# Attention 0 of a fused decoder kernel: moving the transposes of context and input between the fill slots

## The chip, the cores and the metric

The kernel runs on one core of one Trainium2 chip. The metric is device time in microseconds of one execution. Lower is better.

## The reference

The program computes four blocks one after the other on x (16 batches of 100 rows, 256 features) and a context (16 batches of 361 rows, 256 features), all in float32. Block 0 is a decoder layer: causal self-attention with 16 heads, a layer norm, cross-attention to the context, a layer norm, a GELU feed-forward, a layer norm. Blocks 1 and 2 follow with further attentions, feed-forwards and a recurrence, block 3 with a target attention. What the change touches is the first attention of block 0, cut from the reference:

```python
q = jnp.einsum('bsd,hed->bhse', xq, Wq) + bq[None, :, None, :]
k = jnp.einsum('bsd,hed->bhse', xk, Wk) + bk[None, :, None, :]
v = jnp.einsum('bsd,hed->bhse', xv, Wv) + bv[None, :, None, :]
s = jnp.einsum('bhqe,bhke->bhqk', q, k) * (1.0 / math.sqrt(D_MODEL))
if causal:
    s = jnp.where(mask, s, -jnp.inf)
w = jax.nn.softmax(s, axis=-1)
o = jnp.einsum('bhqk,bhke->bhqe', w, v)
...
sa = _mha(q, k, v, m_Wq, ..., causal=True)
x = _ln(x + sa, ln1_g, ln1_b)
```

## The kernel before

The kernel keeps x and the context transposed, features on the partitions, in x_resid and ctx_t. Each of the two 128-feature halves of a tensor is a "part" (c = 0, 1). Batches are worked on one by one, and projections for a group of 4 batches at once (400 columns). The five attentions are called s0, c0, s1, c1, c2; s0 is attention 0.

The order of the work is written out by hand. ORDER gives for each attention the tokens of one batch, and every engine walks through the same string and issues its own share at each token. For batch b in s0: P are the values products of batch b-1 (pe_values), R the scores of batch b with their exp on ScalarE (pe_scores, act_probs), T the "tops", bf16 scores of batch b+1 whose maxima VectorE takes (pe_tops, dve_maxima), V the values projection of b+1, X the turn of the maxima (pe_turn, dve_rows). n0 and n1 are the two halves of batch b-1's normalisation: on ScalarE n0 copies the second heads, on VectorE n0 is two sums, a shuffle and a reciprocal (L1458 to L1465), and n1 the product that writes q_then_o (L1471). GpSimd follows no tokens; it cuts the causal triangle out of the probabilities (L1879) and writes the masked queries (L1869) batch by batch.

F is a fill slot. In s0 a batch has 5 of them, a group 20, numbered from 0. At each F an engine takes one step of several generators that run together (pe_fill, act_fill, dve_fill):

- pe_unload and act_unload turn the context of the group's batches and the x of the next group: TensorE transposes from the staging tile (L460 context, L450 x), ScalarE copies to ctx_t and x_resid (L1021);
- pe_post, from slot POST_AT["s0"] = 3 on, works on the group before: two output projections, then the norm's mean and variance. The first of them waits for n1 of that group's last batch;
- pe_pre, from slot PRE_AT["s0"] on, makes queries and keys of the next group (q0, q1, k0, k1);
- in the last group, pe_open from slot 12 on begins the next attention, c0: queries, keys of batch 0, values and tops, keys of batch 1.

The slots before are, within a group: 1 context 0; 3 x part 0, out 0; 4 context 1, out 1; 6 x part 1, mean; 7 context 2; 9 variance, q0; 10 context 3, q1; 11 k0; 12 k1; 13 to 19 nothing. A context here is both of its parts.

Results of projections, turned maxima and transposes go to a ring of three PSUM banks, 4, 5 and 6; each take waits until the reader of the bank's last content is done. Attention c0 has bank 6 alone for its projections, and pairs of banks (0, 2 and 4) for its tops and keys. The context's staging tile has room for two batches: on SyncE load_ctx waits for the second part of batch b before it loads batch b+2, and load_x waits for the second part of x.

Of the kernel before, what the change touches and what calls it, by code (L numbers as in the profile page):

```python
# [10 lines left out]
ACT = mybir.ActivationFunctionType  # L11
# [4 lines left out]
P = 128  # L16
DC = D // P
GB = 4
NG = B // GB
# [99 lines left out]
for a in ATT.values():  # L119
# [22 lines left out]


ORDER = {
# [5 lines left out]
}  # L150
POST_AT = {"s0": 3, "c0": 0, "s1": 2, "c1": 0, "c2": 6}
PRE_AT = {"s0": 9, "c0": 4, "s1": 4, "c1": 3, "c2": 1}
NORM_OF = {"s0": "n1", "c0": "n2"}
AFTER = {"f0": "c0", "f1": "s1", "f2": "c1"}
FINAL = ("c2", B - 1)
NORM_AFTER = {"f0": "n3", "f2": "r1"}

S0_OPEN = 6
TAIL_AT, CLOSE_AT, LAST_AT = 12, 1, 3

OPEN_AT = ((0, 0, 0, 0), (0, 1, 2, 4), (0, 1, 4, 1))
# [34 lines left out]
def build(nc, book, x_in, ctx_in, vec_in, const_in, src_in, w0_in, w1_in, w2_in, tw_in, out, spill):  # L196
    known = book.known
    with ExitStack() as ctx:
# [98 lines left out]
        def mark(track, point, by=1):  # L297

            counts[track] += by
            book.marks[point] = (track, counts[track])  # L300
            book.totals[track] = counts[track]
            return by
# [141 lines left out]
        def pe_x(pe, g, c, ring):  # L444

            if due(f"x{g}"):
                pe.wait_ge(sems["x_loaded"], at(f"x{g}"))
            bk = ring.take(pe, f"xt{g} {c}", f"xt{g} {c} out")
            for b in range(GB):
                i = nc.tensor.transpose(PS[:, bk, b * S:(b + 1) * S], XST[0:S, b, c * P:(c + 1) * P], IDENT[0:S, 0:S])  # L450
            i.then_inc(products_ready, mark("pe", f"xt{g} {c}"))

        def pe_ctx(pe, b):

            if due(f"ctx{b}"):
                pe.wait_ge(sems[f"ctx{b % 2}_loaded"], at(f"ctx{b}"))
            for c in range(DC):
                bk = lin["s0"].take(pe, f"ct{b} {c}", f"ct{b} {c} out")
                for kc, (k0, kn) in enumerate(KCH):
                    i = nc.tensor.transpose(PS[:, bk, k0:k0 + kn], CST[0:kn, b % 2, kc, c * P:(c + 1) * P], IDENT[0:kn, 0:kn])  # L460
                i.then_inc(products_ready, mark("pe", f"ct{b} {c}"))

        def source(t, g):
            return XN[g] if t == "c2" else X[:, :, cols(g)]
# [169 lines left out]
        def later(slots, part):  # L634
            for _ in range(slots):
                yield
            yield from part
# [66 lines left out]
        def pe_unload(pe, g):  # L704

            for b in range(g * GB, (g + 1) * GB):
                pe_ctx(pe, b)
                yield
                yield
                if b % GB < DC and g + 1 < NG:  # L710
                    pe_x(pe, g + 1, b % GB, lin["s0"])
                yield

        def pe_fill(pe, t, g):

            parts = []
            if t == "s0":
                parts.append(later(1, pe_unload(pe, g)))
            if g or t == "c0":
                parts.append(later(POST_AT[t], pe_post(pe, *((t, g - 1) if g else ("s0", NG - 1)), lin["c2 fill" if t == "c2" else t])))  # L720
            elif t == "s1":
                parts.append(pe_chain(pe, "n3", NG - 1, lin[t]))
            if t == "c2" and g + 1 == NG:
                parts.append(later(TAIL_AT, pe_chain(pe, "r2", 0, lin["c2 fill"])))
            if g + 1 < NG:
                parts.append(later(PRE_AT[t], pe_pre(pe, t, g + 1)))
            elif t == "s0":
                parts.append(later(12, pe_open(pe, "c0")))
            return together(*parts)
# [293 lines left out]
        def act_x(act, g, c):  # L1023
            act_evac(act, f"xt{g} {c}", X[:, c, cols(g)], func=ACT.Copy)
            mark_same(f"s0 in{g} {c}", f"xt{g} {c} out")

        def act_ctx(act, b):
            for c in range(DC):
                act_evac(act, f"ct{b} {c}", CT[:, b, c, :], n=C, func=ACT.Copy)

        def act_query(act, t, g, m, which="q"):
            use = f"{t} {which}{g} {m}"
# [139 lines left out]

        def act_unload(act, g):
            for b in range(g * GB, (g + 1) * GB):
                act_ctx(act, b)
                yield
                yield
                if b % GB < DC and g + 1 < NG:
                    act_x(act, g + 1, b % GB)
                yield  # L1180

        def act_fill(act, t, g):
            parts = []
            if t == "s0":
                parts.append(later(1, act_unload(act, g)))
            if g or t == "c0":
                of, og = (t, g - 1) if g else ("s0", NG - 1)
                if of in NORM_OF:
                    parts.append(later(POST_AT[t] + 3, act_chain(act, NORM_OF[of], og)))
            elif t == "s1":  # L1190
                parts.append(act_chain(act, "n3", NG - 1))
            if t == "c2" and g + 1 == NG:
                parts.append(later(TAIL_AT, act_chain(act, "r2", 0)))
            if g + 1 < NG:
                parts.append(later(PRE_AT[t], act_pre(act, t, g + 1)))
            elif t == "s0":
                parts.append(later(12, act_open(act, "c0")))
            return together(*parts)
# [935 lines left out]
```

## Time and profile before

| | us |
|---|---|
| median of 3 runs | 1598.15 |
| lowest and highest | 1595.85, 1599.1 |
| the profiled execution | 1599.62 |
| its span | 1597.2 |
| PE busy in the span | 1528.3 |
| DVE busy | 775.5 |
| ACT busy | 668.6 |
| POOL busy | 263.0 |

Times in the profile are microseconds from the start of the span. PE is TensorE's matmuls and transposes, PEld its weight loads, DVE VectorE, ACT ScalarE, POOL GpSimd, SPq the queue of SyncE, which issues all DMAs. L435 is line 435 of the kernel; many projections share it. A float32 projection of one 128-feature half is four matmul rows. In timelines instructions of the same line are merged (x4), with the start of the first and the time to the end of the last; matmuls overlap, so prices are best taken from start to start. In brackets stands the idle time of the engine before the row and what ended it. PEclk is the granted TensorE clock as a share of 2.4 GHz: 0.50 is 1.2 GHz, and values between are a mixture of both.

### The profile page before, as it was taken

How to read it: one execution, taken by the hardware profiler on the slowest of the kernel's cores; microseconds unless marked ns; L12 is line 12 of the kernel's file. 1: busy time of each engine (PE TensorE's matmuls, PEld its weight loads, DVE VectorE, ACT ScalarE, POOL GpSimd, SP SyncE). 2: the span in 40 equal slices, each digit the busy share in tenths (PEclk: the TensorE clock that was granted, in tenths of full speed). 3: DMA queues.
4: the chain of work that ended last, by engine and by line, in shares of the span. 5: the costliest groups of instructions: out<-in, count | busy, mean ns of one | idle time of the engine just before them, and what ended most of it. 6: DMA issues, size and time to landing. Idle time of an engine off the chain costs nothing.

```text
span 1597.2 us, 28533 instructions
## 1 busy us (share of the span) xinstructions
PE 1528.3 (96%) x12168; PEld 983.1 (62%) x12168; DVE 775.5 (49%) x1568; ACT 668.6 (42%) x1401; POOL 263.0 (16%) x443
## 2 busy tenths in 40 slices
PE   8899899999999999999999999999899999999997
PEld 7556556666665556555577765555466666655575
DVE  1577667677652235411133342233777777762132
ACT  2455546556564443211243341223554444443243
POOL 1333301010000001000022220000154454410000
PEclk9989989999999999999999999999999999999999
DMA  4311000000000020000020000000000000020032
GB/s 157 101 49 38 20 27 2 2 1 2 2 2 27 0 80 1 21 1 0 0 80 1 1 2 27 0 0 7 27 1 2 2 2 1 2 78 0 0 94 59
DMA packets 19551, 36.83 MB, mean 23 GB/s; under 512 B 2048, under 2 KB 17376, under 8 KB 18272
## 3 DMA queue, kind: packets, MB, share of 16 engines
q1 hardware_dynamic: 19424, 35.01, 6.6%
q8 instruction: 95, 1.56, 0.4%
q14 instruction: 32, 0.26, 0.1%
HBM read 33.36 MB, written 1.64 MB: 22 GB/s over the span
## 4 chain that ended last, share of the span: by engine, by line
PE 83%; DVE 11%; ACT 3%; issue 1%; DMA 1%; POOL 0%; SPq 0%; DVEq 0%; ACTq 0%
PE psum L435 38%; PE psum L792 11%; PE psum L486 8%; PE psum L597 6%; PE psum L558 5%; DVE maxima L1426 3%; PE psum L524 3%; PE psum L897 2%; PE psum L554 2%; DVE denoms L1465 2%; PE psum L925 1%; PE psum L938 1%; PE psum L906 1%; DVE t L1536 1%; PE psum L890 1%
## 5 line engine op out<-in xcount | busy, mean ns | idle before, releaser
L435 PE MATMUL psum<-x_resid,weights 128*128 128x400 f32 x832 | 294.9, 505 | 6.1 <-ACT probs L1100 1.9
L1426 DVE TENSOR_REDUCE maxima<-psum 100x2 f32<-100x722 f32 (+3 forms) x332 | 245.1, 759 | 111.5 <-PE psum L524 95.0
L435 PEld LDWEIGHTS psum<-x_resid,weights 128*128 128x128 f32 x832 | 156.5, 191 | 124.7 <-issue 4.5
L1100 ACT ACTIVATE probs<-psum 128x800 f32<-128x800 f32 (+3 forms) x224 | 168.0, 788 | 106.2 <-PE psum L558 105.0
L792 PE MATMUL psum<-weights 128*128 128x400 f32 x512 | 174.8, 499 | 0.7 <-DVE maxima L1426 0.7
L435 PE MATMUL psum<-weights,ctx_t 128*128 128x256 f32 (+1 forms) x576 | 158.2, 399 | 1.7 <-ACT values L1071 1.0
L792 PEld LDWEIGHTS psum<-weights 128*128 128x128 f32 x512 | 97.2, 190 | 75.1 <-DVE maxima L1426 0.8
L486 PE MATMUL psum<-ctx_t,weights 128*128 128x361 f32 x384 | 140.1, 490 | 1.9 <-DVE weights L1657 0.8
L435 PEld LDWEIGHTS psum<-weights,ctx_t 128*128 128x128 f32 (+1 forms) x576 | 100.4, 186 | 42.5 <-issue 10.8
L1021 ACT ACTIVATE weights<-psum 128x400 f32<-128x400 f32 (+2 forms) x80 | 38.0, 475 | 209.1 <-PE psum L435 209.1
L558 PE MATMUL psum<-q_masked,keys 32*128 32x200 f32 (+4 forms) x1408 | 123.9, 340 | 0.0
L1071 ACT ACTIVATE values<-psum 128x256 f32<-128x256 f32 (+2 forms) x176 | 67.8, 385 | 125.4 <-PE psum L435 90.4
L597 PE MATMUL psum<-probs,values 128*32 128x100 f32 (+5 forms) x3328 | 112.5, 253 | 0.9 <-DVE q_then_o L1484 0.3
L1864 POOL TENSOR_TENSOR q_masked_bf<-q_then_o,ones 128x200 bf16<-128x200 f32 x48 | 25.2, 527 | 507.4 <-ACT q_then_o L1021 445.2
L558 PEld LDWEIGHTS psum<-q_masked,keys 32*128 32x128 f32 (+4 forms) x1408 | 105.7, 184 | 1.2
L1657 DVE TENSOR_TENSOR weights<-psum,weights 128x400 f32<-128x400 f32 x64 | 36.8, 574 | 138.0 <-PE psum L435 119.7
L597 PEld LDWEIGHTS psum<-probs,values 128*32 128x32 f32 (+5 forms) x3328 | 85.4, 114 | 22.1 <-issue 19.2
L486 PEld LDWEIGHTS psum<-ctx_t,weights 128*128 128x128 f32 x384 | 71.2, 198 | 36.0 <-issue 9.3
L1021 ACT ACTIVATE weights<-psum,vectors 128x400 f32<-128x400 f32 x80 | 46.2, 592 | 96.5 <-PE psum L435 95.4
L1437 DVE TENSOR_TENSOR max_rows<-psum,constants 128x400 bf16<-128x400 f32 (+1 forms) x80 | 39.0, 488 | 80.5 <-PE psum L532 79.9
L524 PE MATMUL psum<-keys_bf,q_masked_bf 32*100 32x361 bf16 (+1 forms) x448 | 65.0, 358 | 11.6 <-DVE maxima L1426 6.5
L1536 DVE RECIPROCAL t<-t 128x400 f32<-128x400 f32 x20 | 52.9, 2647 | 45.9 <-ACT t L1121 45.9
(151 smaller groups left out, 2168.1 us busy)
## 6 DMA issues: line engine op xcount, KB each, us to landing
weights<-in_w SPq DMA_DIRECT2D x2, 3072.0 KB, 10.1
staged<-in_ctx SPq DMA_DIRECT2D x32, 128.0 KB, 2.1
values<-in_ctx SPq DMA_DIRECT2D x32, 128.0 KB, 2.1
weights<-in_w SPq DMA_DIRECT2D x3, 1024.0 KB, 4.9
weights<-in_src SPq DMA_DIRECT2D x1, 2368.0 KB, 14.7
weights<-in_w SPq DMA_DIRECT2D x1, 2048.0 KB, 9.0
weights<-in_tw SPq DMA_DIRECT2D x2, 1024.0 KB, 4.9
staged<-in_ctx SPq DMA_DIRECT2D x16, 105.0 KB, 2.3
```

The costliest lines, as they stand in the source:

```text
L435: i = nc.tensor.matmul(PS[0:rows, bk, 0:n], lhs, rhs, start=k == 0, stop=k == len(terms) - 1)
L486: i = nc.tensor.matmul(PS[:, bk + m, 0:C], w(WN[t][1], c, m * P, (m + 1) * P), CT[:, b, c, :], start=c == 0, stop=c == DC - 1)
L524: i = nc.tensor.matmul(PS[0:S, bk + d, 0:C], queries_bf(t, b, i0 + d, c, e), keys_bf(t, b, i0 + d, c, e), start=True, stop=True)
L558: i = nc.tensor.matmul(PS[0:kn, bk + d, m * n:(m + 1) * n], keys_of(t, b, i0 + d, c, a["keys"][kc][0], kn), queries_of(t, b, i0 + d, c), s ...
L597: mm = nc.tensor.matmul(PS[head_rows(t, i, e), bk, o:o + S], lhs, probs_of(t, b, i, c, kc, kn, e), start=kc == 0, stop=kc == lastk)
L792: i = nc.tensor.matmul(PS[:, bk, 0:N], w(wd, k, m * P, (m + 1) * P), hidden[:, k, :], start=k == 0, stop=k == 7)
L1021: nc.scalar.activation(out, PS[0:rows, bank(use), 0:n], func, **kw).then_inc(act_results, mark("act", point or f"{use} out"))
L1071: nc.scalar.activation(dst, src, ACT.Copy).then_inc(act_results, mark("act", f"{use} out"))
L1100: nc.scalar.activation(PT[0:kn, k % PROBS_KEPT, :, 0:n], PS[0:kn, bk:bk + 2, 0:n], ACT.Exp).then_inc(act_results, mark("act", f"{t} p{b} { ...
L1426: nc.vector.reduce_max(top, src, AX).then_inc(dve_results, mark("dve", f"{t} m{b} {j}"))
L1437: nc.vector.tensor_tensor(MB[:, b % 2, 0:n * S].rearrange("p (s q) -> p s q", s=n), PS[:, bank(f"{t} mt{b}"), 0:S].unsqueeze(1).broadcast_ ...
L1536: nc.vector.reciprocal(rs, rs).then_inc(dve_results, mark("dve", f"{n} rs{g}"))
```

## The change

In s0 the third fill slot of a batch moves ahead of n1. The unload generators run over five slots for each batch instead of a first slot left out and three for each batch: the two x parts of the next group are turned in slots 1 and 2 of a group's first batch, and each batch's own context in that batch's slots 3 and 4, one part in each. PRE_AT goes from 9 to 11, so that q0, q1, k0 and k1 stand in slots 11 to 14. The slots of post and of the opening of c0 stay.

```diff
@@ -142,20 +142,23 @@
 ORDER = {
-    "s0": "P0 P1 F n0 R0 R1 F n1 F T0 T1 F F V0 X",
+    "s0": "P0 P1 F n0 R0 R1 F F n1 T0 T1 F F V0 X",
...
-PRE_AT = {"s0": 9, "c0": 4, "s1": 4, "c1": 3, "c2": 1}
+PRE_AT = {"s0": 11, "c0": 4, "s1": 4, "c1": 3, "c2": 1}
...
+SLOTS_S0, CTX_AT, X_AT = 5, (3, 4), ((0, 1), (0, 2))
...
-        def pe_ctx(pe, b):
+        def pe_ctx(pe, b, c):
 
             if due(f"ctx{b}"):
                 pe.wait_ge(sems[f"ctx{b % 2}_loaded"], at(f"ctx{b}"))
-            for c in range(DC):
-                bk = lin["s0"].take(pe, f"ct{b} {c}", f"ct{b} {c} out")
-                for kc, (k0, kn) in enumerate(KCH):
-                    i = nc.tensor.transpose(PS[:, bk, k0:k0 + kn], CST[0:kn, b % 2, kc, c * P:(c + 1) * P], IDENT[0:kn, 0:kn])
-                i.then_inc(products_ready, mark("pe", f"ct{b} {c}"))
+            bk = lin["s0"].take(pe, f"ct{b} {c}", f"ct{b} {c} out")
+            for kc, (k0, kn) in enumerate(KCH):
+                i = nc.tensor.transpose(PS[:, bk, k0:k0 + kn], CST[0:kn, b % 2, kc, c * P:(c + 1) * P], IDENT[0:kn, 0:kn])
+            i.then_inc(products_ready, mark("pe", f"ct{b} {c}"))
...
         def pe_unload(pe, g):
 
             for b in range(g * GB, (g + 1) * GB):
-                pe_ctx(pe, b)
-                yield
-                yield
-                if b % GB < DC and g + 1 < NG:
-                    pe_x(pe, g + 1, b % GB, lin["s0"])
-                yield
+                for slot in range(SLOTS_S0):
+                    for c in range(DC):
+                        if g + 1 < NG and (b % GB, slot) == X_AT[c]:
+                            pe_x(pe, g + 1, c, lin["s0"])
+                        if slot == CTX_AT[c]:
+                            pe_ctx(pe, b, c)
+                    yield
...
-                parts.append(later(1, pe_unload(pe, g)))
+                parts.append(pe_unload(pe, g))
```

The act_ctx, act_unload and act_fill of ScalarE change in the same way.

## Rows read from the trace of the kernel before

**Rows 1.** The page, part 4: the chain that ended last, by engine

```profile
PE 83%; DVE 11%; ACT 3%; issue 1%; DMA 1%; POOL 0%; SPq 0%; DVEq 0%; ACTq 0%
```

**Rows 2.** Table of stretches, one a batch of attention 0 (0-6, 8, 12-15)

```profile
core 0: us, PE busy (x) PEld busy (x) DVE busy (x) ACT busy (x) POOL busy (x), PEclk, DMA share, GB/s
42.19:48.15 5.96, 5.86 (x63) 4.10 (x62) 2.31 (x5) 3.52 (x7) 3.39 (x4) 1.00 0.84 305
48.15:60.15 12.00, 10.24 (x92) 6.63 (x92) 6.31 (x9) 4.62 (x9) 3.51 (x4) 0.72 0.47 153
60.15:70.14 9.99, 9.82 (x96) 5.97 (x95) 5.78 (x9) 6.42 (x13) 3.51 (x4) 1.00 0.12 37
70.14:77.86 7.72, 4.98 (x78) 3.18 (x77) 6.04 (x9) 2.71 (x6) 3.51 (x4) 1.00 0.02 4
77.86:91.66 13.80, 13.80 (x103) 9.14 (x102) 7.47 (x11) 4.48 (x9) 3.51 (x4) 0.63 0.17 55
91.66:101.55 9.89, 9.82 (x101) 6.42 (x100) 6.08 (x11) 7.24 (x13) 3.52 (x4) 1.00 0.28 80
101.55:111.54 9.99, 9.83 (x96) 5.98 (x96) 9.26 (x12) 8.11 (x15) 3.47 (x4) 1.00 0.12 37
...
119.27:130.38 11.11, 11.01 (x103) 7.53 (x102) 7.81 (x11) 4.38 (x9) 3.52 (x4) 0.85 0.24 68
...
157.98:168.78 10.80, 10.68 (x98) 7.15 (x97) 6.49 (x11) 3.86 (x8) 3.52 (x4) 0.84 0.23 69
168.78:177.22 8.44, 8.17 (x93) 5.35 (x92) 6.07 (x11) 6.41 (x11) 3.51 (x4) 1.00 0.01 4
177.22:191.31 14.09, 12.63 (x100) 7.50 (x99) 8.74 (x12) 8.84 (x16) 1.76 (x2) 0.88 0.00 1
191.31:209.75 18.44, 14.64 (x95) 7.72 (x94) 12.05 (x16) 5.08 (x12) 6.76 (x8) 0.72 0.00 1
```

**Rows 3.** Timeline of TensorE in batch 3: start, time, what, idle before

```profile
70.14 0.89 PE L597 MATMUL psum<-probs,values 100*32 100x100 f32 x32
70.97 0.37 PE L554 MATMUL psum<-max_rows,ones_bf 32*100 32x400 bf16 x2
...
73.05 0.51 PE L512 MATMUL psum<-scan_state,ident_bf 100*100 100x400 bf16 x2 [0.81 <-ACT probs L1100]
...
74.59 1.11 PE L435 MATMUL psum<-weights,x_resid 128*100 128x256 f32 x4
77.63 0.30 PE L532 MATMUL psum<-constants,maxima 100*128 100x100 f32 x1 [1.93 <-DVE maxima L1426]
```

**Rows 4.** TensorE in 2 us of batch 4: busy, granted clock

```profile
80.00:82.00 2.00, 2.00 (x11) 0.50 0.00 0
```

**Rows 5.** Timelines of SyncE's queue and of TensorE in batches 0 and 1

```profile
44.26 4.12 SPq L1957 DMA_DIRECT2D staged<-in_ctx  x6
...
52.49 1.47 PE L460 MATMUL psum<-constants,staged 128*128 128x128 f32 x6 [1.76 <-DMA staged<-in_ctx]
```

**Rows 6.** Timeline of TensorE in batches 5 and 6, for prices

```profile
93.68 0.56 PE L450 MATMUL psum<-constants,staged 100*128 100x100 f32 x4
94.08 1.53 PE L435 MATMUL psum<-t,ones_mean 128*128 128x400 f32 x4
...
102.37 0.84 PE L460 MATMUL psum<-constants,staged 128*128 128x128 f32 x6
103.06 1.52 PE L435 MATMUL psum<-x_resid,weights 128*128 128x400 f32 x4
...
105.71 2.95 PE L435 MATMUL psum<-x_resid,weights 128*128 128x400 f32 x8
```

**Rows 7.** Timelines of GpSimd and VectorE: n1 in batches 7 and 12

```profile
114.37 1.76 POOL L1879 TENSOR_SCALAR_AFFINE_SELECT probs<-probs 100x800 f32<-100x800 f32 x2 [2.78 <-ACT probs L1100]
115.97 1.21 DVE L1471 TENSOR_TENSOR q_then_o<-second_heads,denoms 128x200 f32<-128x200 f32 x1
...
163.07 0.39 DVE L1471 TENSOR_TENSOR q_then_o<-second_heads,denoms 128x200 f32<-128x200 f32 x1
```

**Rows 8.** Timelines of TensorE and VectorE in batches 14 and 15

```profile
184.70 2.52 PE L435 MATMUL psum<-x_resid,weights 128*128 128x400 f32 x4 [0.72 <-ACT q_then_o L1021]
...
198.00 2.19 DVE L1471 TENSOR_TENSOR q_then_o<-second_heads,denoms 128x200 f32<-128x200 f32 x1
...
204.42 5.02 PE L486 MATMUL psum<-ctx_t,weights 128*128 128x361 f32 x8 [0.28 <-DVE maxima L1426]
```

More of the change, by code:

```diff
@@ L1025, in act_x, with act_ctx @@
             mark_same(f"s0 in{g} {c}", f"xt{g} {c} out")
-        def act_ctx(act, b):
-            for c in range(DC):
-                act_evac(act, f"ct{b} {c}", CT[:, b, c, :], n=C, func=ACT.Copy)
+        def act_ctx(act, b, c):
+            act_evac(act, f"ct{b} {c}", CT[:, b, c, :], n=C, func=ACT.Copy)
         def act_query(act, t, g, m, which="q"):
@@ L1174, in act_unload @@
             for b in range(g * GB, (g + 1) * GB):
[L1175 to L1180, printed above, removed]
+                for slot in range(SLOTS_S0):
+                    for c in range(DC):
+                        if g + 1 < NG and (b % GB, slot) == X_AT[c]:
+                            act_x(act, g + 1, c)
+                        if slot == CTX_AT[c]:
+                            act_ctx(act, b, c)
+                    yield
         def act_fill(act, t, g):
@@ L1184, in act_fill @@
             if t == "s0":
-                parts.append(later(1, act_unload(act, g)))
+                parts.append(act_unload(act, g))
             if g or t == "c0":
```

## Prediction

> **What bounds the kernel now.** I read the page first, then a table of stretches cut at the batches of attention 0, then the timelines of TensorE, VectorE, ScalarE and GpSimd inside them. The page's chain of the work that ended last is 83% PE and 11% DVE [rows 1]: TensorE's stream sets the time wherever it is full, VectorE where it runs dry. The change touches only attention 0, 167.56 us from 42.19 to 209.75; I cut it where TensorE starts a batch's values products (tokens P0 P1) [rows 2]. Two kinds of batch stand there.
>
> Batch 3 (and 7 and 11, 7.73 and 7.72 us) has no fill at all: TensorE is busy for 4.98 of 7.72 us. It waits 0.81 us for the first exp before the next batch's tops (T0), and 1.93 us for the maxima before the turn (X) [rows 3]. What sets 7.72 is a loop through VectorE: values, ScalarE's copies of the second heads, n0 with its reciprocal, n1, two maxima, turn, values. Batches 2, 5 and 6 are the other kind: TensorE 9.82 or 9.83 of 9.89 or 9.99 us, that is full.
>
> Two losses follow. The DVE loop leaves the array idle in batches 3, 7 and 11, and in batches 4, 8 and 12, which follow them, the mean granted clock is 0.63, 0.85 and 0.84, part of each at the lower level of 1.2 GHz: 80 to 82 us shows 0.50 [rows 2, 4]. And in batch 1 TensorE waits 1.76 us for the DMA of the context, then runs at the lower clock too (0.72) [rows 2, 5]. That load is issued at 44.26, while the queues move 305 GB/s (the 2 MB of ff weights go first), and wanted eight us later [rows 5].
>
> **Prices at the full clock.** From start to start, less the waits: values 0.83, scores 1.27, tops 1.54, V 1.11, X 0.23, which is batch 3's 4.98 [rows 3]. In a full stream the tail of V runs beside the next row, so I count the bare batch at 4.8. Both context parts of a batch together 0.69 (102.37 to 103.06), an x part 0.40 (93.68 to 94.08), a projection of 400 columns 1.40 (105.71 to 108.50 for two) [rows 6]. Out, mean, var, q0, q1, k0, k1 are all such projections. Batch 5 checks it: 4.8 + 0.4 + 1.4 + 0.7 + 1.4 + 1.4 = 10.1 against 9.89.
>
> **Part 1, the DVE order.** On TensorE and ScalarE "F n1 F" and "F F n1" are the same stream, since n1 is an instruction of VectorE alone. On VectorE the third slot of a batch (slots 2, 7, 12, 17 of a group) holds fill only in slot 17 of the last group, the second maxima of the next attention. Everywhere else this edit costs and brings nothing.
>
> **Part 2, what each batch then holds.** No instruction is added or removed; 16 context pairs, 6 x parts and 12 projections change place. The fill per batch of a group becomes: first, x x, context, out out; second, mean, context, var; third, q0 q1, context, k0 k1; fourth, context.
>
> Batch 0: x1 comes, a pair goes: 5.96 - 0.7 + 0.4 = 5.7. Batch 1 has only its own pair, 4.8 + 0.7 = 5.5, less than the DVE loop, so it costs 7.7 instead of 12.00; its context was loaded at the start, and the DMA wait is gone. The loads move too: SP waits for the second part of batch b before it loads b+2, so ctx2 is issued at about 47 and read at about 60, ctx3 and x2 behind it at about 55 and read 13 us later or more, against the 8 us that were too few. What is queued on SP behind them is only the next loads. Batch 2: 4.8 + 4 x 1.4 + 0.7 = 11.1, with no gap, since q0 and q1 cover the wait for exp. Batch 3: 7.7 as before; the pair (0.7) lies in the 1.93 us wait for the maxima.
>
> Batch 4 (8 and 12 alike): the bare sum with two x parts, a pair and two outs is 4.8 + 0.8 + 0.7 + 2.8 = 9.1. But the first out needs n1 of the batch before. The context used to stand ahead of it in a full stream; now, at full clock, TensorE arrives about 4.9 us after the batch's start, while n1 ends 5.6 us after it (batch 7: 111.54 to 115.97 + 1.21) [rows 7]. So 0.9 us of waiting: 10.0, instead of 13.80, 11.11 and 10.80. Its other bound is 0.1, with n1 as short as in batch 12 (163.07, 0.39 us); GpSimd's select lies beside n1 in batch 7 [rows 7], and nothing moves it away from n1 in 4 and 8, so I take 0.9 and keep 3 x 0.8 = 2.4 us for the range. In batch 12, without x parts, the wait for exp stands there instead, so it is 10.0 as well. Batch 5 (9 and 13): q0 leaves; batch 13 has just this content and takes 8.44 now. Batch 6 (and 10): as batch 2, 11.1. VectorE's scale of the norm (a 2.6 us reciprocal and two products) is done inside it, some 1.5 us before TensorE reaches X. q0 and q1 are read out two slots later, so GpSimd's masks of the next group's first batch wait about 1 us more; nobody reads them before the fourth batch's tops.
>
> Batches 14 and 15 hold the opening of attention 1, whose linear ring is one bank, 6. Counting the takes of the ring 4, 5, 6, the second part of ctx14 and the first of ctx15 fall on bank 6. In batch 14 the pair of ctx15 leaves from ahead of the scores, but its own second part now stands between q1 and the keys and must wait until ScalarE has read q1 (there is such a wait ahead of q1 now, 0.72 us) [rows 8]. Bounds from -0.8 (pair gone, warm clock) to +0.9 (a wait of 0.85 at the low clock, behind it the keys); I take 0, 14.1, as both pull about alike. In batch 15 the first part of ctx15 waits for ScalarE's copy of v1 on bank 6, v2 waits for the copy of the part, the second part goes ahead of the fourth tops, and the keys of batch 1, now at 204.42 behind a chain of maxima, move by 1 to 1.5 us. The order edit gives something back: one maxima comes ahead of n1, which takes 2.19 us at 198.00 beside GpSimd's masks [rows 8]. Together +1.4, 19.8; bounds 0 and +2.5. Nothing hides this: the next thing late is batch 1's keys.
>
> **The sum**: group 0 5.7 + 7.7 + 11.1 + 7.7 = 32.2 (35.7 before); groups 1 and 2 10.0 + 8.4 + 11.1 + 7.7 = 37.2 each (41.4 and 38.7); group 3 10.0 + 8.4 + 14.1 + 19.8 = 52.3 (51.8). Total 158.9 against 167.6: -8.7 us. From the profiled execution's 1599.62 that is 1590.9; the median of the runs is 1.5 us lower, and some of that may be batch 4's long low-clock stretch being shorter in other runs, so I don't subtract it. Forecast **1591.0 us**.
>
> **Where a rule bears.** n1 takes 1.21 us in batch 7 beside GpSimd's select and 0.39 in batch 12 [rows 7]. The Trainium skill's SBUF — State Buffer, Who interferes with whom, says that a VectorE instruction with two SBUF inputs contends with a GpSimd one that reads SBUF, and n1 has two such inputs. By that rule, the trace agrees. It would make the wait ahead of the first out depend on the chance order of the two engines; the sum by it is 1591.0 with the contention and 1588.6 without.
>
> **Rivals.**
> Clock. The forecast has full clock after batches 1, 3, 7 and 11. TensorE's gaps there shrink from 0.81 + 1.93 to about 0.8 + 1.2 us. For a fall: batch 14 shows the clock going down (0.88) with gaps of only about 0.9 and 0.7 us in it. Against: batches 5, 9 and 13 stay at 1.00 with small gaps. If it falls after all four as it does after batch 11, batches 4, 8 and 12 cost 0.8 more each (10.80 against 10.0) and the full batch 2 about 1.7: 4.1, so 1595.1. Chance 0.20, half of it on either side of the bound. The skill's TensorE: Matmul & The Clock Gate, Part 1, says that the throttled state is the default and activity releases it; by that rule less idle time can only help, but it doesn't say that 1.2 us is little enough.
>
> Slower. Long cold stretches: batch 4 took 13.80, 4.5 us over its sum at full clock (9.3: 4.8 + two 0.7 + 0.4 + two 1.4), since the lower clock held through nearly all of it. If each of the four lulls is followed by such a stretch, 4 x 4.4 = 17.6 is added: 1608.5. It decides from three such stretches on (13.2 over the forecast, 1604). Against it: two of three lulls of 1.93 us cost under 2 us. Chance 0.05.
>
> The change does less than it says. If only the DMA wait and its cold stretch go (12.00 to 7.7 and 9.99 to 11.1, -3.2), and elsewhere the fill lands on batches that are full anyway, while the DVE loop still rules the emptied ones: 1596.4. Chance 0.08.
>
> Opening of attention 1. Both waits on bank 6 at their upper bounds, +0.9 and +1.1 over the forecast, and the low clock over keys and values another 1.5: 1594.5. Chance 0.12.
>
> **Chances and range.** Forecast 0.55 (1586 to 1594.5). A kernel of this spread can be told from no change from about 0.2%, 3.2 us. Faster by more, under 1594.95: 0.55 + 0.12 + 0.08 = 0.75; within: 0.12 + 0.08 = 0.20; slower 0.05. The range goes down from 1591.0 by the 2.4 of n1, by 0.8 and 1.4 (14 and 15 at their lower bounds) and by the 1.5 of the median, to 1585, to 1597.5, which takes in the clock rival with 14 and 15 at their upper bounds.
>
> **What would show it.** In the profile after, cut the same way: batch 1 near 7.7 and no row of TensorE waiting for DMA staged; batches 4, 8 and 12 near 10.0 with a wait of about 0.9 for VectorE's n1 ahead of the first out; 2, 6 and 10 near 11.1 with TensorE full; 3, 7 and 11 unchanged at 7.7 with a wait for the maxima of about 1.2; clock 1.00 from 48 us to about 185. Wrong it would be if batches 3, 7 and 11 got longer (the pair is on the loop after all), if the clock in batch 2 or 4 is under 0.9, or if 14 and 15 grow by over 3 us together.

## The result, and the profile after

The changed kernel takes **1586.81 us** (median of 20 runs, 1582.49 to 1592.77); the kernel before, run beside it, 1593.32 us (20 runs, 1586.54 to 1602.77). The ratio is **0.9946, interval [0.9932, 0.9961]**. It is faster, by 8.6 us if the ratio is applied to 1593.32 and by 6.5 us between the two medians. The profiled execution took 1585.96 us (span 1584.0), against 1599.62 and 1597.2.

The three runs shown with the kernel before are the first of these twenty. Their median was 1598.15; the other seventeen brought it down to 1593.32. That matters below.

The chain of the work that ended last, by engine, on the page of the changed kernel:

```profile
PE 84%; DVE 11%; ACT 4%; issue 1%; DMA 0%; POOL 0%; SPq 0%; DVEq 0%; ACTq 0%
```

Nothing new bounds the kernel [rows 1]; only TensorE's stream got shorter. The same table of stretches as in [rows 2], one row a batch of attention 0, cut where TensorE starts the values products of each batch. Batches 0 to 6, 8, and 12 to 15:

```profile
core 0: us, PE busy (x) PEld busy (x) DVE busy (x) ACT busy (x) POOL busy (x), PEclk, DMA share, GB/s
40.99:46.40 5.41, 5.38 (x60) 3.82 (x59) 2.31 (x5) 3.19 (x6) 3.34 (x4) 1.00 0.81 291
46.40:54.13 7.73, 5.59 (x85) 3.79 (x84) 6.13 (x9) 3.91 (x8) 3.57 (x5) 1.00 0.46 165
54.13:64.93 10.80, 10.80 (x101) 6.79 (x100) 5.30 (x9) 6.25 (x12) 3.42 (x4) 1.00 0.24 67
64.93:72.65 7.72, 5.58 (x85) 3.78 (x84) 6.04 (x9) 4.03 (x9) 3.52 (x4) 1.00 0.20 61
72.65:82.51 9.86, 9.15 (x101) 6.01 (x100) 7.22 (x11) 4.04 (x8) 3.51 (x4) 1.00 0.11 33
82.51:90.94 8.43, 8.30 (x92) 5.32 (x92) 6.08 (x11) 6.23 (x11) 3.52 (x4) 1.00 0.19 53
90.94:101.74 10.80, 10.80 (x101) 6.79 (x100) 8.73 (x12) 8.94 (x17) 3.73 (x4) 1.00 0.22 67
...
109.46:119.32 9.86, 9.14 (x100) 6.01 (x99) 7.22 (x11) 4.04 (x8) 3.52 (x4) 1.00 0.12 33
...
146.28:157.79 11.51, 9.99 (x93) 6.15 (x92) 7.30 (x11) 3.25 (x6) 3.51 (x4) 0.85 0.09 29
157.79:166.21 8.42, 8.31 (x92) 5.32 (x91) 6.08 (x11) 6.24 (x11) 3.52 (x4) 1.00 0.19 52
166.21:178.76 12.55, 11.18 (x100) 6.64 (x99) 8.73 (x12) 8.97 (x17) 1.97 (x2) 1.00 0.01 2
178.76:199.76 21.00, 16.83 (x100) 8.93 (x99) 11.07 (x16) 6.28 (x15) 6.76 (x8) 0.67 0.00 1
```

Batch by batch, with the omitted rows filled in from the same view (us):

| batch | 0 | 1 | 2 | 3, 7, 11 | 4, 8, 12 | 5, 9, 13 | 6, 10 | 14 | 15 | attention 0 |
|---|---|---|---|---|---|---|---|---|---|---|
| before | 5.96 | 12.00 | 9.99 | 7.72, 7.73, 7.72 | 13.80, 11.11, 10.80 | 9.89, 9.89, 8.44 | 9.99, 9.99 | 14.09 | 18.44 | 167.56 |
| predicted | 5.7 | 7.7 | 11.1 | 7.7 | 10.0 | 8.4 | 11.1 | 14.1 | 19.8 | 158.9 |
| after | 5.41 | 7.73 | 10.80 | 7.72, 7.72, 7.73 | 9.86, 9.86, 11.51 | 8.43, 8.44, 8.42 | 10.80, 10.79 | 12.55 | 21.00 | 158.77 |

Attention 0 gave 8.8 us, the 8.7 that was forecast. The rest of the span difference of 13.2 us is not in what was changed: the time before attention 0 is 1.2 shorter (42.19 and 40.99), and all that follows it takes 1384.24 instead of 1387.45, 3.2 less, with the same instructions.

TensorE's timeline after, in batches 3 and 4 (start, time, what, idle before it):

```profile
67.83 0.51 PE L514 MATMUL psum<-scan_state,ident_bf 100*100 100x400 bf16 x2 [0.81 <-ACT probs L1102]
69.37 0.84 PE L462 MATMUL psum<-constants,staged 128*128 128x128 f32 x6
...
72.41 0.31 PE L534 MATMUL psum<-constants,maxima 100*128 100x100 f32 x1 [1.33 <-DVE maxima L1429]
...
78.34 1.61 PE L438 MATMUL psum<-q_then_o,weights 128*128 128x400 f32 x4 [0.71 <-DVE q_then_o L1474]
```

The line numbers are two or three higher than before. The context pair (69.37) now lies in what was one wait of 1.93 us for the maxima [rows 3], of which 1.33 is left; the wait for exp is still 0.81. In batch 4 the first out projection now waits 0.71 us for n1, where 0.9 was foreseen. No row of TensorE waits for the DMA of the context any more [rows 5].

### The profile page after: what moved, and what is told of

It is laid out like the page before. It is cut to its first block, busy times and chain, and to the rows that moved or that the text cites. A ratio compares the mean times of both kernels' runs of the same rounds, so it can differ in the third digit from the quotient of the medians.

```text
span 1584.0 us, 28538 instructions
## 1 busy us (share of the span) xinstructions
PE 1513.9 (96%) x12168; PEld 972.5 (61%) x12168; DVE 772.3 (49%) x1568; ACT 669.0 (42%) x1401; POOL 263.6 (17%) x443
## 4 chain that ended last, share of the span: by engine, by line
PE 84%; DVE 11%; ACT 4%; issue 1%; DMA 0%; POOL 0%; SPq 0%; DVEq 0%; ACTq 0%
PE psum L438 39%; PE psum L795 11%; PE psum L488 8%; PE psum L599 6%; PE psum L560 5%; DVE maxima L1429 3%; PE psum L526 3%; PE psum L900 2%; DVE denoms L1468 2%; PE psum L556 2%; PE psum L928 1%; PE psum L941 1%; PE psum L909 1%; DVE t L1539 1%; PE psum L893 1%; DVE q_then_o L1474 1%
## 5 line engine op out<-in xcount | busy, mean ns | idle before, releaser
L560 PE MATMUL psum<-q_masked,keys 32*128 32x200 f32 (+4 forms) x1408 | 119.4, 328 | 0.0
L560 PEld LDWEIGHTS psum<-q_masked,keys 32*128 32x128 f32 (+4 forms) x1408 | 102.2, 177 | 0.8
L526 PE MATMUL psum<-keys_bf,q_masked_bf 32*100 32x361 bf16 (+1 forms) x448 | 64.8, 358 | 11.4 <-DVE maxima L1429 6.3
```

Source lines behind the costliest of these rows:

```text
L526: i = nc.tensor.matmul(PS[0:S, bk + d, 0:C], queries_bf(t, b, i0 + d, c, e), keys_bf(t, b, i0 + d, c, e), start=True, stop=True)
L560: i = nc.tensor.matmul(PS[0:kn, bk + d, m * n:(m + 1) * n], keys_of(t, b, i0 + d, c, a["keys"][kc][0], kn), queries_of(t, b, i0 + d, c), s ...
```

## The experiments

All times in the batch tables are read as above. **The clock theory**: the schedule is worth something in itself, and most of the gain is TensorE's clock, kept up because the wait in batches 3, 7 and 11 is partly filled. **The rival**: single parts of the change (the DMA wait, the shift of queries and keys, the place of n1) carry the gain.

**Both kernels again, unchanged** (e1, e2).

> The kernel before once more, unchanged, for the level. Theory: the schedule of attention 0 repeats to 0.1 us wherever the clock is full (batches 2, 3, 5, 6, 7 at 9.99, 7.72, 9.89, 9.99, 7.73 us), and what differs between executions is how long the 1.2 GHz stretches after batches 1, 3, 7 and 11 last; the 167.56 us of attention 0 would come out anywhere from 160 to 170, and batch 4 nearer 11 than 13.80. Rival: the whole kernel runs slower or faster by a common factor; then the full-clock batches differ as well.

> The changed kernel once more, unchanged. Theory: batches 0 to 11 of attention 0 repeat to 0.1 us (5.41, 7.73, 10.80, 7.72, 9.86, 8.43, 10.80, 7.72, 9.86, 8.44, 10.79, 7.73), since no low-clock stretch falls there; only batches 12, 14 and 15 differ by the place of such stretches. Rival: low-clock stretches fall after batches 3, 7 and 11 in some executions and batches 4 or 8 show 11 us or more.

Before again: 1597.61 us against 1596.49 for the kernel before beside it, ratio 1.0 [0.9978, 1.0023]. After again: 1584.37, ratio 0.9928 [0.9906, 0.9949]. The gain stands; with the runs of e12 (below, 0.995) its three ratios lie from 0.9928 to 0.995. In the second profile of the changed kernel batches 1 to 11 repeat to 0.1 us, and batch 12 took 11.35; but batch 0 took 8.28 us at 0.59 instead of 5.41 at 1.00. Low clock in batch 0 stands in 7 of the 16 profiles, with either schedule. Two rows of the table of stretches of before again, batches 1 and 4:

```profile
49.36:57.88 8.52, 8.09 (x93) 5.58 (x92) 6.25 (x9) 4.73 (x10) 3.52 (x4) 0.90 0.43 113
...
75.72:90.75 15.03, 15.03 (x103) 10.16 (x102) 6.67 (x11) 4.48 (x9) 3.52 (x4) 0.57 0.17 50
```

Batch 1 took 8.52 us here and not 12.00: batch 0 had itself run at the lower clock (9.33 us), so the context had landed by the time it was wanted. The 4.3 us that batch 1 gained between the two profiles is therefore not a fixed price. Batch 4 fell again, 15.03 us at 0.57; batches 8 and 12 as well (11.20 and 13.56). The fall behind batches 3, 7 and 11 recurs in the kernel before, with a varying price.

**The shift of queries and keys undone** in the changed kernel (e3).

```
-PRE_AT = {"s0": 11, ...
+PRE_AT = {"s0": 9, ...
```

> The changed kernel with PRE_AT of attention 0 back at 9: queries and keys of the next group in slots 9 to 12 as before. Theory (TensorE is full in the groups' middle batches, so a projection of 1.40 us costs the same in either, and costs nothing only inside the VectorE loop of 7.7 us): batch 1 stays 7.7 with q0 inside the loop, batch 2 falls from 10.80 to 9.7; batches 5 and 9 rise from 8.43 to 9.8, batches 6 and 10 fall from 10.80 to 10.0; in all -1.1 + 2 x 0.6 = +0.1 us for attention 0. Rival (the two-slot shift carries part of the gain): attention 0 longer by 2 us or more.

1588.70 us, ratio 0.995 [0.993, 0.997]. Batches 5 and 6 took 9.78 and 10.91, together 20.69 us, against 19.23 with the shift; in group 0, batch 2 gained 1.2 (9.61 for 10.80). TensorE's timeline of e3 in batch 6:

```profile
99.89 0.53 PE L462 MATMUL psum<-constants,staged 128*128 128x128 f32 x3 [0.40 <-ACT keys L1024]
...
100.86 1.11 PE L438 MATMUL psum<-weights,x_resid 128*100 128x256 f32 x4 [0.44 <-ACT keys L1024]
```

Two waits that I had not expected: ScalarE's copies of the keys stand behind its part of the norm, in the same slots, so the ring has no free bank for the context. The shift is worth 1.5 us in each of groups 1 and 2 and costs 1.2 in group 0: with batch 12 at equal clock that is some 1.7 us in all. By the ratios (0.995 and 0.9928, with intervals that overlap) that is not resolved.

**The last group's contexts back in their old slots** (e4).

```
+def ctx_at(b):
+    n = b % GB
+    if b >= B - GB:
+        return (1 + 3 * n, 1 + 3 * n)
+    return (SLOTS_S0 * n + 3, SLOTS_S0 * n + 4)
```

> The changed kernel with the context of the last group alone turned where it was before, both parts in slots 1, 4, 7 and 10, ahead of the opening of attention 1. Theory (bank 6 of the ring serves two masters, and the context of batch 15 stands between the tops of the opening): batch 15 goes from 21.00 to about 18.4, batch 14 from 12.55 to 12.4 at full clock or 14.1 at the lower one, batch 12 about 10.3; attention 0 shorter by 1 to 3 us. Rival (batch 15 is long only because the clock is low in it, 0.67): batch 15 stays at 20 to 21.

Batches 14 and 15 took 12.41 + 18.25 = 30.66 us, where the changed kernel has 33.55. The table's row of batch 15:

```profile
185.45:203.70 18.25, 14.23 (x95) 7.65 (x94) 10.77 (x16) 5.08 (x12) 6.77 (x8) 0.72 0.00 1
```

So the last group's contexts in their new slots cost 2.9 us in this pair of profiles, 2.75 of it in batch 15. Not all of that is waiting for the bank. The two waits around the context's first part are 0.84 us together (rows below, in the part on the prediction); the two parts of context 15 are themselves now turned in this batch, at the lower clock, and the low clock lasts longer (mean 0.67 against 0.72). In e13 below, batch 15 has the instructions of the changed kernel and took 19.46 us at 0.74, so a good part of the 2.9 us comes and goes with the clock. The runs, 1588.53 us and 0.9938 [0.9914, 0.9962], don't show that gain: its profiled execution took 1389.20 us behind attention 0, 4.8 more than e2's, at a mean clock of 0.99 instead of 1.00. The waits are shown by the rows; what they are worth in the kernel's time was not measured by themselves (the version at the end makes three moves at once).

**The ff weights' load put behind group 0's context loads**, in the kernel before (e5), to take away the DMA wait of batch 1 and leave the rest.

```
-            load_weights(sp, "ff", ...)
             for g in range(NG):
...
+                if g == 0:
+                    load_weights(sp, "ff", ...)
```

> The kernel before, with one load moved: the 2 MB of feed-forward weights go out on SyncE's queue behind the context loads of the first group instead of ahead of them. Theory (batch 1 lost 1.76 us to the DMA and more to the low clock after it): no wait for DMA in batch 1, which falls from 12.00 (8.52 beside a 9.33 batch 0 in the second trace) to the 7.7 of the VectorE loop; batches 2 to 15 as before, batches 4, 8 and 12 still followed by low clock. About 3 to 4 of the 8.7 us of the change from this alone: ratio 0.998. Rival (the wait is cover for something else): batch 1 stays over 9.

Batch 1, from the table of stretches of e5:

```profile
48.10:55.84 7.74, 7.30 (x93) 4.94 (x92) 6.14 (x9) 4.79 (x10) 3.52 (x4) 1.00 0.57 147
```

7.74 us and no wait, as expected, in that profile; but 1594.34 us over 12 runs and a ratio of 0.9992 [0.9972, 1.0013]. Even the low end of that interval is half of the change's gain. Taking the DMA wait away alone leaves the low clock behind batches 3, 7 and 11 (batches 4, 8 and 12 took 11.85, 10.93 and 14.75 us at 0.86, 0.84 and 0.56 here).

**The order of VectorE's n1 alone** (e6), in the kernel before.

```
-    "s0": "P0 P1 F n0 R0 R1 F n1 F T0 T1 F F V0 X",
+    "s0": "P0 P1 F n0 R0 R1 F F n1 T0 T1 F F V0 X",
```

> The kernel before with the ORDER edit alone, the third fill slot ahead of n1. Theory: batches 0 to 14 of attention 0 as before (9.99, 7.72, 9.89 and so on at full clock); in batch 15 one maxima stands ahead of n1, and n1 is no longer 2.19 us long beside GpSimd's masks; batch 15 shorter by 0.5 to 1 us against 18.44 or 17.99. Rival: the order of the slots carries part of the gain in every batch.

This was run once (1599.67 us, beside a median of 1594.62 for the kernel before), so its time says nothing; the rows do. Every batch took what it took before to 0.1 us, batch 15 18.45 (18.44 before), where 0.5 to 1 less was expected. VectorE's timeline of e6 in batch 15:

```profile
199.27 0.91 DVE L1426 TENSOR_REDUCE maxima<-psum 100x2 f32<-100x722 f32 x1 [0.43 <-PE psum L524]
200.10 0.84 DVE L1471 TENSOR_TENSOR q_then_o<-second_heads,denoms 128x200 f32<-128x200 f32 x1
201.86 5.00 DVE L1426 TENSOR_REDUCE maxima<-psum 100x2 f32<-100x722 f32 x6 [0.92 <-PE psum L524]
```

n1 is shorter in its new place, 0.84 us (200.10) against 2.19 [rows 8], and then VectorE stands idle for 0.92 us, because the tops of the next maxima aren't there yet. The edit shortens an instruction and gains nothing.

**The shift of queries and keys alone**, PRE_AT 9 to 11 in the kernel before (e7 run once, e9 again with 12 runs).

> The kernel before with PRE_AT at 11 alone. Theory: per group the second batch loses a 1.40 us projection and the third gains one, 9.89 to 8.7 and 9.99 to 11.1; the fourth batch stays empty at 7.7 and the clock falls behind it as before (batches 4, 8 and 12 at 11 us or more). Attention 0 within 1 us of the kernel before apart from the length of the low-clock stretches. Rival: this part alone removes the low clock.

> The kernel before with PRE_AT at 11 alone, a second trace, now timed. In its first trace batches 3, 7 and 11 had their full wait of 1.93 us and yet the clock stayed at 1.00 in batches 4, 8 and 12 (10.52 us each). Theory A (whether the clock falls hangs on where the wait lies in time, and that differs between executions): this trace shows low clock in at least one of batches 4, 8, 12, and the ratio over the executions is near 0.997. Theory B (queries and keys two slots later keep the clock up by themselves): batches 4, 8, 12 at 10.52 and 1.00 again, ratio near 0.994.

e7's row of batch 4, and TensorE's timeline from the turn of batch 3 to the first out of batch 4:

```profile
75.94:86.46 10.52, 9.70 (x103) 6.32 (x102) 7.22 (x11) 4.37 (x9) 3.52 (x4) 1.00 0.25 72
```

```profile
75.70 0.31 PE L532 MATMUL psum<-constants,maxima 100*128 100x100 f32 x1 [1.94 <-DVE maxima L1426]
...
81.63 1.61 PE L435 MATMUL psum<-q_then_o,weights 128*128 128x400 f32 x4 [0.68 <-DVE q_then_o L1471]
```

This refuted a part of my theory and a number of my prediction. The wait of 1.94 us was there, and yet the clock stayed at 1.00 in batches 4, 8 and 12, in both profiles. So the wait makes a fall likely and does not force it. And at full clock these batches take 10.52 or 10.53 us in the old schedule, not the 9.3 of my sum: the wait for n1 (0.68) is in the old order too. The time: e7's one run took 1587.54 us, but e9's twelve run from 1583.66 to 1598.05 with a median of 1594.72, ratio 0.9988 [0.9967, 1.0009]. Three of the twelve are near 1584 to 1586, the others at 1591 to 1598; both profiles happened to fall near the low end. So e9's ratio is near the 0.997 of its theory A, though its trace shows no fall in batches 4, 8 and 12, and far from the 0.994 of theory B. The shift alone is no gain that can be told, and one profile shows one execution, not the kernel's level. Why the clock held in these two executions stays open.

**The gap opened again, in the changed kernel** (e10): the context pairs of batches 3, 7 and 11 move from slots 18 and 19 of their group, ahead of the turn, to slot 14, the last slot of the batch before; the rest of the stream stays.

```
+    if n == GB - 1 and b < B - 1:
+        return (14, 14)
+    return (SLOTS_S0 * n + 3, SLOTS_S0 * n + 4)
```

> The changed kernel, with the context of the fourth batch of groups 0 to 2 turned in the third batch (slot 14), so that batches 3, 7 and 11 are empty again, with a wait of 1.93 instead of 1.33 us for the maxima. At full clock this costs 3 x 0.65 = 2 us: batches 2, 6 and 10 at 11.4 to 11.5. Theory (the longer wait lets the clock fall): low clock in batches 4, 8 or 12, attention 0 at 163 us or more, ratio 0.996 or worse. Rival (the clock is kept by something else in the changed kernel): batches 4 and 8 at 9.86 and 1.00, attention 0 near 161, ratio 0.994.

**The same, with the gap filled by work of no use** (e13): three transposes of a weight into a bank of the ring, twice a group, in slots 18 and 19 of groups 0 to 2. Nothing reads them.

```
+        def pe_warm(pe, g):
+            for slot in range(5 * GB):
+                if slot >= 18 and g + 1 < NG:
+                    c = slot - 18
+                    bk = lin["s0"].take(pe, f"warm{g} {c}", f"warm{g} {c}")
+                    for kc, (k0, kn) in enumerate(KCH):
+                        i = nc.tensor.transpose(PS[:, bk, k0:k0 + kn], w("sq", c, 0, P, rows=kn), IDENT[0:kn, 0:kn])
+                    i.then_inc(products_ready, mark("pe", f"warm{g} {c}"))
+                yield
```

> The kernel with the gap opened (contexts of batches 3, 7 and 11 turned in batches 2, 6 and 10), and in the place they left, slots 18 and 19 of groups 0 to 2, a pair of transposes of the same form that read a weight and that nobody reads: work added for nothing. Up to batch 3's gap the stream is the same as with the gap open, so the place of things in time doesn't differ. Theory (TensorE's work in the gap keeps the clock): batches 4 and 8 at about 9.9 and 1.00 instead of 14.67 and 13.44, attention 0 near 163 instead of 172.91, ratio 0.996. Rival (the clock hung on where batch 3's end lies in time, which the pair in the third batch shifts): low clock as with the gap open, ratio 1.001.

Batches 3 and 4, first in e10's table of stretches, with the wait ahead of the turn from its TensorE timeline, then the same from e13:

```profile
66.54:74.39 7.85, 5.10 (x79) 3.22 (x78) 6.04 (x9) 3.21 (x7) 3.52 (x4) 0.95 0.05 15
74.39:89.06 14.67, 14.67 (x100) 9.74 (x99) 6.67 (x11) 4.09 (x8) 3.52 (x4) 0.56 0.09 26
```

```profile
74.03 0.43 PE L543 MATMUL psum<-constants,maxima 100*128 100x100 f32 x1 [1.94 <-DVE maxima L1440]
```

```profile
69.78:77.51 7.73, 5.58 (x84) 3.78 (x83) 6.04 (x9) 3.21 (x7) 3.52 (x4) 1.00 0.05 14
77.51:87.37 9.86, 9.14 (x100) 6.01 (x99) 7.22 (x11) 4.04 (x8) 3.52 (x4) 1.00 0.10 33
```

```profile
77.27 0.31 PE L543 MATMUL psum<-constants,maxima 100*128 100x100 f32 x1 [1.34 <-DVE maxima L1452]
```

Batch 4 holds the same hundred matmuls in both: 14.67 us at 0.56, and 9.86 at 1.00. Batches 8 and 12 took 13.44 and 12.78 with the gap open, 9.86 and 11.55 with it filled. The runs agree: e10 1597.18 us, ratio 1.0012 [0.9999, 1.0025]; e13 1591.72, 0.9961 [0.9947, 0.9974]. With the gap open, the changed kernel has no gain left. Not all of that is clock: e10's batches 2, 6 and 10 came to 12.27, 12.27 and 12.26, where 11.4 to 11.5 was expected, since the moved pairs collide with the keys on the ring and wait 0.55 us for ScalarE. Against the changed kernel's 10.80 that is 4.4 us lost at full clock. e13 has this too, so that only the step between the two ratios, 0.5% or about 8 us, is the gap's.

One thing of e13's expectation did not come true. The place in time did differ between the two profiles: e13's batches 0 and 1 ran at low clock (8.86 and 8.71 us), and its batch 3 starts at 69.78, e10's at 66.54. The two profiles alone therefore leave the rival of the place in time open. Against it stand the ratios, and a count over all 16 profiles, in which batches 3, 7 and 11 lie at many different times. Behind a wait of 1.93 or 1.94 us batches 4, 8 and 12 were under full clock in 15 of 21 cases (all six others in e7 and e9). Behind one of 1.33 or 1.34 us they were in 4 of 27, each time batch 12. Batches of one profile are not independent of each other, so this is a tendency and not a law.

**The gap filled in the kernel before** (e14): the same unread pair, and nothing of the change.

> The kernel before with nothing but such an unread pair of transposes added in slots 18 and 19 of groups 0 to 2. Theory: batches 4 and 8 fall to about 10.5 at full clock, batch 12 too unless the clock falls by its own wait for n1; batch 1 with its DMA wait stays; the median falls by 3 to 6 us although work is added, ratio 0.996 to 0.998. Rival (the change gains by the order of the stream and not by the clock): no gain or 1 to 2 us slower, ratio 1.000 or 1.001.

Its batches 3 and 4 in the table, and its TensorE timeline in batch 3:

```profile
70.90:78.62 7.72, 5.57 (x84) 3.77 (x83) 6.04 (x9) 2.71 (x6) 3.52 (x4) 1.00 0.01 4
78.62:89.15 10.53, 9.70 (x102) 6.32 (x101) 7.22 (x11) 4.37 (x9) 3.52 (x4) 1.00 0.24 72
```

```profile
75.34 0.84 PE L721 MATMUL psum<-constants,weights 128*128 128x128 f32 x6
...
78.39 0.30 PE L532 MATMUL psum<-constants,maxima 100*128 100x100 f32 x1 [1.34 <-DVE maxima L1438]
```

1590.17 us against 1595.91, ratio **0.996 [0.9948, 0.9972]**, with the clock at 1.00 from batch 1 to batch 14 in the profile. (The DMA wait of batch 1 was expected to stay; batch 0 ran at 0.60 here, and batch 1 took 7.74 us without one. That part of the profile is luck and not the fill's doing.) Eighteen matmuls that compute nothing bring about 6 us (0.004 x 1595.91), some three quarters of what the change brings by its first ratio (0.9946; by its second, 0.9928, a little over half). The half of the clock theory that is about the clock holds. That the schedule is worth something in itself at full clock does not; the next part has the sum.

**A version from these readings** (e8, e11), beside the changed kernel a third time (e12): contexts of the last group in slots 2, 3, 8 and 11, away from the opening's bank, both parts of the others in the fourth slot, and group 0's queries and keys in their old place.

```
+    if b >= B - GB:
+        return ((2, 2), (3, 3), (8, 8), (11, 11))[n]
+    return (SLOTS_S0 * n + 3, SLOTS_S0 * n + 3)
...
-                parts.append(later(PRE_AT[t], pe_pre(pe, t, g + 1)))
+                parts.append(later(PRE_AT[t] - 2 * (t == "s0" and g == 0), pe_pre(pe, t, g + 1)))
```

> The changed kernel, with three more moves: both parts of a context in slot 3 of its batch, ahead of the first out; q0 to k1 of the second group back in slots 9 to 12 (that group has no norm chain beside them); in the last group the contexts in slots 2, 3, 8 and 11, none of them behind the opening of attention 1. Theory: batch 2 9.6 instead of 10.80; batches 4 and 8 9.5 instead of 9.86; batch 12 9.7; batch 14 about 11.8 instead of 12.55; batch 15 about 18.3 instead of 21.00: attention 0 near 152.8, 6 us shorter than the changed kernel, ratio to before near 0.989. Rival (what is taken away in attention 0 is given back in low clock later, as when the last group's contexts alone were put back): ratio 0.993 as the changed kernel.

> The tuned version once more, beside the changed kernel on the same chip. Theory: attention 0 near 153 again (batches 2, 4, 14 at 9.6, 9.53, 12.0), median 3 to 5 us below the changed kernel's. Rival: the 16.53 us of batch 15 was a lucky clock, attention 0 is 155 to 157 and the medians differ by 1 to 2 us.

> The changed kernel a third time, beside the tuned version. Theory: batches 0 to 11 repeat to 0.1 us apart from the opening batch, attention 0 from 158 to 162 by the low-clock stretches in batches 0, 12 and 15; ratio to before 0.992 to 0.996. Rival: the ratio of 0.9946 and the 0.9928 of the second set were of different chips and it falls outside.

The version took 1581.63 us, ratio 0.9914 [0.9888, 0.9939], and again 1581.28, 0.9926 [0.9901, 0.995]; the changed kernel beside the latter 1585.74, 0.995 [0.9931, 0.9969]. It is the fastest here, 4.5 us under the median of the changed kernel run beside it (1585.74 - 1581.28). Attention 0 took 152.79 us in e8, as expected, and 154.21 in e11; in e12 157.05, which is below its expected 158 to 162, because batches 0 and 12 ran at full clock. The version's last batch (e8's table):

```profile
176.56:193.09 16.53, 11.92 (x94) 6.74 (x93) 10.71 (x16) 5.08 (x12) 6.76 (x8) 0.90 0.00 1
```

16.53 us and, in e11, 17.96, where the changed kernel has 21.00, 20.92 and 20.94. That is the largest part (3 us between e12 and e11, at a mean clock of 0.67 and 0.82, so some of it is clock). Batch 2 at 9.61 gives 1.2, batches 4, 8 and 12 give 0.3 each and batch 14 gives 0.5.

## Why the prediction was partly right and partly wrong

The forecast of 1591.0 us was a gain of 2.3 us on the level that the kernel before has over 20 runs. It was 6.5 to 8.6. The range, 1585 to 1597.5, holds the 1586.81.

**The step that failed is the level to which the sum was applied.** "From the profiled execution's 1599.62 that is 1590.9; the median of the runs is 1.5 us lower [...] so I don't subtract it." The sum itself, -8.7 us, is 8.7/1599.62 = 0.54%: a ratio of 0.9946, which is what was measured. But the execution from which it was taken sits near the top of a spread of 16 us (1586.54 to 1602.77), 6.3 us over the median, and the three runs at hand were all high too. Applied to 1593.32, the same sum gives 1584.6. I had argued that long stretches of low clock may be shorter in other runs, and then left the argument out of the number. It would have cut both ways: a part of the 8.7 is that same clock. What the runs showed in place of the 1599.62 is a level of 1593.32, spread over 16 us by low clock that comes and goes.

**That 158.77 met 158.9 is in part luck.** In that profile batch 12 was 1.5 us over its sum, batch 14 1.5 under and batch 15 1.2 over, and the batches of four projections 0.3 under each; the errors cancel. The changed kernel's other two profiles have 161.43 and 157.05 us for attention 0.

**Batches 0 to 3, 5 to 7, 9 to 11, 13: right**, each within about 0.3 us of the sum, and batches 2, 6 and 10, with four projections each, are full as said (10.80 of 10.80 us busy).

**Batches 4 and 8: right in size, wrong in part of the working.** They took 9.86 against 10.0 (batch 12 11.51, of which below). The wait for n1 was 0.71 for 0.9; the prediction's own two times, 5.6 and 4.9 us after the batch's start, are 0.7 apart, and 9.1 + 0.7 is 9.8. Wrong was the price of the old batch at full clock. The terms given for it (4.8 + two 0.7 + 0.4 + two 1.4) add to 9.4, not 9.3, and it is 10.52 (e7, e14), since the wait for n1 stood there too. So the fall of batch 4 cost 3.3 us (13.80 - 10.52) and not 4.5, and the "slower" rival was priced too high.

**Where the gain is from: the weight on the clock was too small.** Put the quickest time that any profile shows of each batch of the old schedule side by side (5.96, 7.74, 9.99, 7.72, then 10.52, 9.89, 9.99, 7.72 twice, then 10.52, 8.42, 12.41, 17.99) and the sum is 157.0 us. The changed kernel's e12, with no batch below full clock up to batch 14, takes 157.05. At equal clock and without the DMA wait the rearrangement is worth about nothing; what it gives in batch 0 (0.5), in 5 and 9 (1.5 each) and in 4, 8 and 12 (0.7 each) it gives back in 2, 6 and 10 (0.8 each) and in 15 (3.0, part of it clock, which is low there on both sides). Its worth is that the array is not idle for 1.93 us in three places, and that batch 1 does not wait for its load. My part by part sum had this as one effect of several. e10, e13 and e14 show that the gaps are most of it; e5 shows that the DMA wait alone is not. The list of quickest times is a sum of pieces from several executions, not a measured run.

**The clock rival (0.20) came true in one batch of four at most.** Of batches 2, 4 and 8 none was under 1.00 after the change; batch 12 was low in two profiles (11.51 at 0.85, 11.35 at 0.85) and at full clock in a third (9.85). The fill of batch 11 is that of 3 and 7, and why batch 12 alone falls was not tried. (The chances count this rival unevenly: halved, as the text says, it makes them 0.77 and 0.18 and not 0.75 and 0.20.)

**Batches 14 and 15: together near, singly off.** I had 14.1 and 19.8, measured were 12.55 and 21.00. Batch 14 ran at 1.00 instead of 0.88 and came out below its lower bound of 13.3: in the old schedule too it takes 12.42 at full clock (e1), so its low clock had cost 1.7 us, which my bounds did not hold. TensorE's timeline of the changed kernel in batches 14 and 15:

```profile
172.61 1.61 PE L438 MATMUL psum<-x_resid,weights 128*128 128x400 f32 x4 [0.26 <-ACT q_then_o L1024]
174.90 0.53 PE L462 MATMUL psum<-constants,staged 128*128 128x128 f32 x3 [0.69 <-ACT q_then_o L1024]
...
186.20 0.83 PE L462 MATMUL psum<-constants,staged 128*128 128x128 f32 x3 [0.28 <-ACT values L1073]
187.60 2.04 PE L438 MATMUL psum<-weights,ctx_t 128*105 128x256 f32 x4 [0.56 <-ACT ctx_t L1024]
```

The three waits on bank 6 are the ones named: 0.69 between q1 and the keys, where q1's own shrank from 0.72 to 0.26; 0.28 and 0.56 around the context in batch 15. Without them batch 15 takes 18.25 in e4. I had the waits, took +1.4 for the batch and it was +2.6, at the upper bound of 2.5. What I had too small is the rest: the pair's own work at the lower clock, and more of that clock (0.67 instead of 0.72, and 0.74 in e13). What the order edit was to give back is not there (e6).

**n1 beside GpSimd.** After the change n1 took 1.21 us in batches 4, 8 and 12, as the prediction took it, and TensorE's wait for it was 0.71 us in each. The other bound rested on batch 12 of the kernel before, 0.39 us [rows 7]; but GpSimd's select ran beside n1 there too. Its row, and from the changed kernel n1 in batch 12 and n1 of the last batch, which falls into attention c0 with GpSimd idle around it (from 188.3 to 208.6 us):

```profile
162.34 1.88 POOL L1879 TENSOR_SCALAR_AFFINE_SELECT probs<-probs 100x800 f32<-100x800 f32 x2 [5.74 <-ACT probs L1100]
```

```profile
150.70 1.21 DVE L1474 TENSOR_TENSOR q_then_o<-second_heads,denoms 128x200 f32<-128x200 f32 x1
...
204.19 0.37 DVE L1474 TENSOR_TENSOR q_then_o<-second_heads,denoms 128x200 f32<-128x200 f32 x1
```

The Trainium skill (SBUF — State Buffer, Who interferes with whom) says that a VectorE instruction with two SBUF inputs contends with a GpSimd instruction that reads SBUF. The trace agrees as far as it goes: alone n1 takes 0.37 us, and in attention 0 of both profiles every n1 of 0.71 us or more, up to 2.19 [rows 8], overlaps work of GpSimd. Overlap alone does not make it long, as batch 12 of the kernel before shows; what decides between 0.39 and 1.21 us was not tried.

**What stays open.** The part of the kernel behind attention 0 has the same instructions in all fourteen experiments and took from 1384.23 to 1389.20 us in their profiles, with more low clock where it took longer. Of the 13.2 us between the spans of before and after, 3.2 are of that kind, and 1.2 lie ahead of attention 0, where the profiles have anything from 38.36 to 44.57 us. Whether the schedule of attention 0 has a hand in it was not tried.

## What to carry to other kernels

Where TensorE runs dry for a moment and its granted clock is low behind it, look first for work to put into the gap, even work of no use: the price of such a gap here was not the wait but the batch behind it. Give a forecast as a difference and put it on the median of many runs; when the runs of a kernel spread by 1%, a profiled execution is a sample of it, and losses that come and go with the clock belong into the range with the share of runs that have them. At the hand-over from one stage to the next, count who takes which bank: transposes that cost no wait through a whole stage waited there.

## What the runs showed of the hardware that I had not expected

Added matmuls that nobody reads made a kernel faster: ratio 0.996 with 18 of them, six in each of three gaps, which cut the wait left there from 1.94 to 1.34 us. A gap of 1.94 us is followed by a low clock in some executions and not in others: the batch behind it took 13.80, 15.03 and 14.67 us in three profiles (0.63, 0.57, 0.56), and 10.52 at 1.00 in two others with the same wait. And low clock early can hide a DMA wait later: where batch 0 took 9.33 us (e1), batch 1 no longer waited and took 8.52 instead of 12.00; in e14, behind a batch 0 of 8.59 us, it took 7.74.
